# Causal attention on one core: the values' products of a key tile's two halves, and of the last two key tiles, are issued in one visit

## The reference, cut to what matters

```
x = x + attention(layernorm(x))
Q, K, V = heads(x @ WQ), heads(x @ WK), heads(x @ WV)      # 16 heads of 8
score = Q @ K.T / sqrt(8) + mask                            # keys after the query masked
score = exp(score - max(score))                             # maximum over the keys of a query
out = (score / sum(score)) @ V
return out @ WO
```

## Time and profile before

| what | value |
|---|---|
| time, median of 3 runs | 3489.86 us (3482.51 to 3497.15) |
| profiled execution, its own time | 3486.21 us |
| its span | 3484.3 us |
| mean granted TensorE clock | 0.925 |
| PE busy | 2833.4 us (81%) |
| DVE busy | 2478.2 us (71%) |
| ACT busy | 1756.8 us (50%) |
| first and last exponential of causal attention (L1417) | 805.5 and 1349.7 us from the span's start |

### The profile page before, as it was taken

How to read it: one execution, slowest core, us unless ns; L and a number is a source line. 1 busy time by engine, 2 the same in 40 slices (tenths; PEclk the granted TensorE clock), 3 DMA queues, 4 the chain that set the end, 5 groups by cost and what they waited for, 6 DMA issues and landing times. The chain is left out here.

```text
span 3484.3 us, 62796 instructions
## 1 busy us (share of the span) xinstructions
PE 2833.4 (81%) x22143; PEld 1662.3 (48%) x22143; DVE 2478.2 (71%) x4050; ACT 1756.8 (50%) x3569; POOL 1837.0 (53%) x1184
## 2 busy tenths in 40 slices
PE   3677468568999995999999993677677599999998
PEld 1211257443444442677667752223222277757774
DVE  5599646558777763777577755698599777767774
ACT  3544125134556553677467732544444277737762
POOL 3499211130111101888188822698299598729871
PEclk9699678779999997999999996899899899999999
DMA  3355000042222210112112210343054112211121
GB/s 90 79 162 151 8 7 1 8 116 69 38 44 38 44 24 24 38 40 47 30 36 44 43 25 5 109 158 121 31 169 157 56 40 44 45 24 42 42 45 40
DMA packets 176158, 203.21 MB, mean 58 GB/s; under 512 B 108358, under 2 KB 122396, under 8 KB 175388
## 3 DMA queue, kind: packets, MB, share of 16 engines
q1 hardware_dynamic: 175868, 199.41, 22.2%
HBM read 138.36 MB, written 9.44 MB: 42 GB/s over the span
## 5 line engine op out<-in xcount | busy, mean ns | idle before, releaser
L319 POOL TENSOR_TENSOR arena<-arena 128x1024 f32<-128x1024 f32 x192 | 451.3, 2351 | 61.1 <-DVE arena L336 34.0
L1450 DVE TENSOR_REDUCE causal_peak_parts<-psum 128x1 f32<-128x512 f32 (+3 forms) x608 | 375.9, 658 | 114.9 <-PE psum L1308 69.6
L2047 POOL TENSOR_TENSOR arena<-arena,w_minus_half 128x16 f32<-128x16 f32 x128 | 372.5, 2910 | 97.0 <-DVE arena L1954 97.0
L1417 ACT ACTIVATE arena<-psum 128x512 f32<-128x512 f32 (+1 forms) x608 | 304.0, 597 | 229.5 <-PE psum L1330 106.7
L1889 ACT ACTIVATE arena<-psum,arena 128x128 f32<-128x128 f32 x1024 | 277.8, 382 | 252.8 <-DVE arena L1963 252.8
L336 DVE TENSOR_TENSOR_SCAN arena<-psum,arena 128x1024 f32<-128x1024 f32 x160 | 364.6, 2280 | 27.9 <-POOL arena L319 27.9
L289 ACT ACTIVATE psum<-arena,w_A 128x1024 f32<-128x1024 f32 x192 | 214.5, 1118 | 248.5 <-DVE arena L336 211.4
L2054 POOL TENSOR_TENSOR arena<-arena 128x1024 f32<-128x1024 f32 x124 | 292.4, 2358 | 12.6 <-DVE arena L1948 12.6
L1734 PE MATMUL psum<-w_layer_wqkv,arena 128*128 128x512 f32 x512 | 262.7, 638 | 5.7 <-DVE arena L1948 3.7
L262 PE MATMUL psum<-arena,m_sel 96*128 96x512 bf16 x384 | 117.4, 388 | 180.6 <-DVE arena L351 153.0
L1959 DVE COPY arena<-psum 128x512 f32<-128x512 f32 x128 | 88.5, 691 | 238.0 <-PE psum L1746 238.0
(11 more groups left out here) (331 smaller groups left out, 6620.7 us busy)
## 6 DMA issues: line engine op xcount, KB each, us to landing
arena<-scan_rows_large SPq DMA_DIRECT2D x128, 512.0 KB, 3.7
arena<-arena SPq DMA_DIRECT2D x256, 130.0 KB, 2.6
arena<-scan_rows_small SPq DMA_DIRECT2D x128, 256.0 KB, 3.8
arena<-causal_parts SPq DMA_DIRECT2D x288, 64.0 KB
causal_parts<-arena SPq DMA_DIRECT2D x8, 768.0 KB, 9.0
arena<-Z SPq DMA_DIRECT2D x128, 32.0 KB, 1.9
arena<-Z SPq DMA_DIRECT2D x32, 128.0 KB
arena<-in_c_pads SPq DMA_DIRECT2D x4, 896.0 KB
```

What stands on the lines that cost most here:

```text
L319: pool.tensor_tensor(inputs[:, s % 2], b_lane[:, s % U], du(*runs[o]), ALU.mult).then_inc(input_up.sem, 1)
L1417: act.activation(PT[:, kt % 2, heads[0]:heads[0] + len(heads), lo:hi], place, ACT.Exp, scale=SCALE).then_inc(probs.sem, 1)
L1450: dve.tensor_reduce(part[:, heads[0]:heads[0] + len(heads), qt, half:half + 1].rearrange("p h a -> p (h a)"), place[:, 0:len(heads) * size ...
L2047: pool.tensor_tensor(RN[:, s4, :], SS[:, s4, :], k.minus_half[:, 0:2 * HEADS], ALU.pow).then_inc(rn_in.sem, 1)
```

## The change

`follow` now gives lists of key tiles. A key tile's two halves are one item whose cost is the sum of both, and key tiles 6 and 7 of the round before are one item after S2; nothing follows S1 any more. `body` loops over the key tiles and halves of an item. The whole of the columns is unchanged, but ring steps that fell due between the two halves now stand ahead of both.

```diff
-        follow = {min(after[kt] + 2, N2 - 1): kt for kt in range(TPB - 2)} | {1: TPB - 2, 2: TPB - 1}
+        follow = {min(after[kt] + 2, N2 - 1): [kt] for kt in range(TPB - 2)} | {2: [TPB - 2, TPB - 1]}
...
-                kt = follow[i]
-                items += [("values", kt, half, 4 * ((half + 1) * BANK - max(kt * P, half * BANK))) for half in range(kt // 4, 2)]
+                items.append(("values", follow[i], None, sum(4 * (SEQ - kt * P) for kt in follow[i])))
...
-                        if kind == "values" and at < TPB - 2:
-                            values(at, half, r)
-                        elif kind == "values" and before:
-                            values(at, half, r - 1)
+                        if kind == "values":
+                            for kt in at:
+                                for side in range(kt // 4, 2):
+                                    if kt < TPB - 2:
+                                        values(kt, side, r)
+                                    elif before:
+                                        values(kt, side, r - 1)
```

## The result

The changed kernel takes 3509.58 us (median, 3502.59 to 3518.23), the kernel before 3490.86 in the same runs: 1.0061 times as long, 95% interval 1.0044 to 1.0077. The forecast was 3509. The span of the profiled execution grew from 3484.3 to 3505.5 us, and the stage, from the first to the last exponential, from 544.19 (805.50 to 1349.69) to 562.73 us: 18.5 of the 21.2. The other 2.7 us lie outside it, where the change touches nothing.

The account below looks back on a forecast made before the run. PE sets the pace, tied to DVE and ACT in rings of three banks. Middle rounds at +1.41 us and the outer rounds sum to +19.0 us: 3505.2 for the profiled execution, 3509 as median, range 3489 to 3519.

Parts of the forecast that it names:

- What a visit costs: On PE, each merge of two visits saves 0.24 us where PE does not have to wait instead.
- upper bound of 18.4 us: Over the stage, the most that 76 merges could gain, if only the saved switches counted.
- The start of a round: V6, now behind S2, R2 and R3, starts later; ACT's first exponentials and S7 move with it: +0.68 us a round.
- The wait before S3: At a round's start, a new wait of about 0.6 us, since S3 uses the bank of the delayed first exponential.
- The ring before V0 to V3: Bunched ring steps wait for DVE to empty three banks: +0.37, +0.15, 0 and +0.21 us a round.
- The sum: Whole stage: +1.41 us a middle round, thirteen of them 18.3; round 0 +0.7, round 14 -0.4, round 15 +0.4; together +19.0.
- The waits for DVE: PE's waits for DVE before the first pass grow from 26.6 us by about 13 times 1.7.
- The rivals: Other outcomes for the total: slack covers it, 3471 (chance 0.08); half the cost, 3486 or 3497 (0.19); clock falls, 3525 and up (0.05).
- the clock: Rival: new waits in each round lower PE's granted clock, 1.2 us or more each, 3525 and up; chance 0.05.
- neither half of the cost was absorbed: Rival: only the round's start costs (3486) or only the ring waits cost (3497), the other being absorbed; chance 0.19.

Follow-up runs that it names:

- more_early: Kernel before with only the cost of S3 to S7 in the order's list counted two and a half times, halves separate: round 33.48 us, ratio 0.9955.
- ring_behind_more_early: ring_behind with the cost of S3 to S7 in the order's list counted two and a half times: round 32.51 us, ratio 0.9907 to the kernel before.
- start_only: Kernel before with only V6 and V7 joined after S2, halves of key tiles 0 to 3 separate: round 35.37 us, ratio 1.0035.
- v7_with_v6_after_s1: Kernel before with V7 moved up to V6's place after S1, halves separate: round 34.68 us, ratio 1.0001.
- ring_behind_v6_with_v5: ring_behind with V6 in one visit with V5 at its own round's end, V7 after S1: round 33.12 us, ratio 0.9942 to the kernel before.
- half reduces: Kernel before and changed kernel, each with reduce L1450 reading half of each score row: rounds 34.29 and 34.87 us, ratios 0.9988 and 1.0015 to the kernel before.
- after_half_reduce: Changed kernel with reduce L1450 reading only half of each score row: round 34.87 us, ratio 1.0015 to the kernel before.
- ring_behind: Kernel before with halves of key tiles 0 to 3 joined, the second half's ring steps behind the pair: round 34.18 us, ratio 0.9984.
- halves_only: Kernel before with only halves of key tiles 0 to 3 joined, both halves' ring steps ahead of them: round 35.48 us, ratio 1.0030.

## Why the prediction was right

- *What a visit costs* (0.24 us): confirmed where nothing waits, by more_early against ring_behind_more_early (0.97 for four). The upper bound of 18.4 us could not be reached in the change's order.
- *The start of a round* (+0.68): measured +0.68 in the change and +0.68 in start_only. That the visit saved disappears in the wait is shown by v7_with_v6_after_s1, and that V6's place is what moves the chain by the copy and S7 in ring_behind_v6_with_v5. The wait before S3 was foreseen as 0.62 (1011.30 to 1011.92). S3 comes 2.99 us behind the last exponential where 2.98 was written, and V6 1.57 (1053.68) as written, so the wait is 0.63; the 0.79 of the row is another quantity.
- *The ring before V0 to V3* (0.37, 0.15, 0, 0.21): measured 0.39, 0.18, 0.01, 0.23. The half reduces show the first three to be the reduce's length; that the last is the addition's is argued from its wait. Each term is 0.01 to 0.03 short, which was not resolved. R10 to R11 itself took 0.59 us, and 0.59 (0.22 and a wait of 0.37) was written.
- *The sum*: from the first exponential to the last exponential of round 0, 31.08 us instead of 30.02, +1.1 where 0.7 was written. Rounds 1 to 13, +19.4 where 18.3 was. Round 14, 30.86 instead of 31.25: -0.4 as written. Round 15, 30.53 instead of 32.03: -1.5 where +0.4 was. Together the stage's 18.5, so the total of 19.0 is so close by luck: two errors of 1.5 and 1.9 us cancel. Nearly all of round 15's is the clock. All these kernels wait about 2 us there for the transfer of the maxima, and the granted clock is low for some us around or behind the wait, for longer in some executions than in others. Round 15, from last exponential to last exponential, in the kernel before, the changed one and v7_with_v6_after_s1:

```profile
1317.66:1349.69 32.03, 27.33 (x200) 10.13 (x200) 2.96 (x4) 19.57 (x40) 0.40 (x1) 0.89 0.03 7
```

```profile
1336.19:1366.71 30.52, 25.00 (x197) 10.14 (x200) 2.96 (x4) 19.46 (x39) 0.40 (x1) 0.94 0.03 7
```

```profile
1316.54:1347.07 30.53, 25.41 (x197) 9.97 (x200) 2.95 (x4) 19.47 (x40) 0.40 (x1) 0.94 0.03 7
```

v7_with_v6_after_s1 has the old order in this round but for V7's place, and at the same clock it takes the same 30.53 as the changed kernel; start_only, at 0.89, takes 32.16 against the 32.03 of the kernel before. So the change costs round 15 about nothing where +0.4 was written, and the 1.5 us are not the change's. Without round 15 the stage lost 20.0 us, where 18.6 was written.

- *The waits for DVE* before the first pass: 37.0 us before (26.6, and 5.4, 2.9 and 2.1 in smaller rows of the table) and 50.1 after, 13 more where 22 was written. The 26.6 that the prediction takes for waits of PE are idle time of the weight loads, which need not hold up a product: in the kernel before, shortening every reduce took only 0.40 a round, some 5 us in 13 rounds. So the table names the waits but does not price them.
- *The rivals*: the clock was 1.00 in every middle window; neither half of the cost was absorbed.

What was least sure was how the result would stand to 0.5%, since the forecast of 19.0 us lay only 1.6 us above it; it came out at 0.61%, with an interval that reaches under 0.5%.

## What to carry to other kernels

In a stage with a fixed period, walk the busiest engine's list through one period with the starts and durations of the trace, and let each instruction begin at the later of two times: its own engine's, and its bank's. Here this gave the change's terms to within 0.03 us each, and the rounds tried afterwards to within about 0.1, but for after_half_reduce (0.17 off) and ring_behind, where only a range of 0.5 was given. Merging visits pays its full price only where no new wait arises. Moving the work that stood between them ahead of the merged visit makes long rows of it (0.79 lost with rows of 4, 4, 3, 4, 0.21 gained with 4, 3, 3, 2); moving it behind was better (0.51 gained in ring_behind), though at V2 a wait took the gain there too. A ring of three buffers holds a row of three quick producers at most, and only if the slow consumer has emptied it; here the fourth waited 0.4 us, and before V0 the third 0.24 as well. And whatever releases another engine's chain (V6 here) must not move back to make a merge possible.

## What was not expected of the hardware

Two executions of different programs repeat a round to 0.01 us: 34.68 or 34.69 in all 13 rounds of the kernel before and of v7_with_v6_after_s1. So a difference of a few hundredths in a round can be read from a single profile, while a dozen whole runs leave some 4 us open (the width of halves_only's interval is 9 us). And nearly the same wait in front of round 15, 1.9 to 2.4 us, was followed by two outcomes: over the whole of round 15 the granted clock was 0.89 in four of the 12 traces and 0.94 in the other eight. Between the kernel before and v7_with_v6_after_s1 that was 1.5 us, as much as the change costs in a middle round. Waits of 1.0 us in each middle round left the clock at 1.00.
